# An audio tower on one core: centring as a matmul, experts two ahead, and a written order of all steps

## What is computed

```python
h = ln(patches @ W.T + b) * gamma + beta                 # 64 clips x 45 tokens x 64
h = h + attention(ln(h))                                 # 8 heads of 8, 4 kv heads, rotary, causal
h = h + sum_e cw[:, e] * (gelu(ln(h) @ W1[e] + b1[e]) @ W2[e] + b2[e])   # 8 experts, top 2 of a softmax gate
h = h + rwkv(ln(h))      # r, k, v, decay w, a, gate g from mixes with the token before; a state recurrence
                         # S = S*decay + (S @ -kk)(kk*a)^T + v k^T over 45 tokens; group norm; o*g @ W_o
h = h + ffn(ln(h))       # relu(x @ Wi.T + bi), two layers with a shared and a routed 128x128 matrix per clip
```

## Time and profile before

| | before |
|---|---|
| median of 3 runs (365.42 to 366.38) | 366.18 us |
| the profiled execution, its own time | 367.88 us |
| its span, first to last instruction | 365.1 us |
| PE matmul, busy | 316.4 us, 87% |
| DVE, busy | 214.6 us, 59% |
| ACT, busy | 192.1 us, 53% |
| POOL, busy | 138.8 us, 38% |
| mean granted TensorE clock | 0.949 |

### The profile page before, as it was taken

One profiled execution on the slowest core, in us unless ns is written; L12 is line 12 of the kernel. 1 busy time (PEld: TensorE's weight loads), 2 busy tenths in 40 slices (PEclk: granted clock), 3 DMA queues, 4 the chain that ended last, 5 costly groups with the idle time before them and its releaser, 6 DMA issues.

```text
span 365.1 us, 11788 instructions
## 1 busy us (share of the span) xinstructions
PE 316.4 (87%) x4888; PEld 221.0 (61%) x4888; DVE 214.6 (59%) x438; ACT 192.1 (53%) x378; POOL 138.8 (38%) x142
## 2 busy tenths in 40 slices
PE   4999899999998799999748895897787879969996
PEld 1446567766865544445324453897686869934784
DVE  4669987787556753332597389983566603285102
...
DMA packets 20556, 14.80 MB, mean 41 GB/s; under 512 B 2328, under 2 KB 19352, under 8 KB 20376
## 3 DMA queue, kind: packets, MB, share of 16 engines
...
...
HBM read 13.32 MB, written 0.74 MB: 38 GB/s over the span
## 4 chain that ended last, share of the span: by engine, by line
PE 62%; DVE 20%; ACT 9%; POOL 5%; issue 4%; DVEq 0%; POOLq 0%
PE PS L786 57%; PE PS L849 5%; DVE arena L591 2%; DVE arena L574 2%; POOL arena L342 2%; ACT arena L379 2%; ACT arena L376 2%; DVE arena L737 1%; POOL arena L338 1%; ACT arena L488 1%; DVE arena L731 1%; POOL arena L337 1%; DVE PS L523 1%; ACT arena L492 1%; ACT arena L371 1%
## 5 line engine op out<-in xcount | busy, mean ns | idle before, releaser
L786 PE MATMUL PS<-arena,K 128*128 128x360 f32 (+2 forms) x576 | 143.5, 503 | 21.3 <-DVE arena L591 6.7
L786 PE MATMUL PS<-arena 128*45 128x45 f32 (+5 forms) x3392 | 119.7, 223 | 18.1 <-issue 7.7
L786 PEld LDWEIGHTS PS<-arena,K 128*128 128x128 f32 (+2 forms) x576 | 74.8, 183 | 84.7 <-issue 22.8
L786 PEld LDWEIGHTS PS<-arena 128*45 128x45 f32 (+4 forms) x3392 | 102.4, 129 | 36.0 <-issue 13.4
L321 POOL TENSOR_TENSOR arena<-arena 128x360 f32<-128x360 f32 x32 | 29.4, 950 | 57.8 <-DVE arena L698 57.8
L698 DVE TENSOR_TENSOR arena<-PS,arena 128x360 f32<-128x360 f32 x32 | 16.9, 531 | 28.3 <-PE PS L786 26.7
L403 ACT COPY arena<-PS 128x360 f32<-128x360 f32 x32 | 14.8, 467 | 24.2 <-PE PS L849 24.2
L347 POOL TENSOR_TENSOR arena<-arena 128x360 f32<-128x360 f32 x4 | 4.4, 1111 | 56.3 <-DVE arena L582 56.3
L421 ACT ACTIVATE arena<-PS,K 128x720 f32<-128x720 f32 x32 | 24.9, 861 | 0.0
L310 POOL TENSOR_TENSOR arena<-arena,K 128x360 f32<-128x360 f32 x32 | 24.1, 789 | 0.0
L488 ACT ACTIVATE arena<-arena,K 128x360 f32<-128x360 f32 x8 | 4.3, 589 | 35.1 <-DVE arena L768 35.1
...
## 6 DMA issues: line engine op xcount, KB each, us to landing
WG<-wr SPq DMA_DIRECT2D x64, 64.0 KB, 1.9
arena<-wr SPq DMA_DIRECT2D x64, 64.0 KB, 1.8
...
```

The costliest lines, as they stand in the source:

```text
L786: return nc.tensor.matmul(o, l, r, start=start, stop=stop)
```

## The change

- A constant matrix `cent` (identity minus `mean`) is added to the first group of constants. `mean.k` multiplies by it, so that bank 0 holds the centred values; ACT squares from the bank, and the multiplication in `var.k` reads the bank. The DVE subtraction is gone.
- `hid.i` waits for `y_mul` of expert i-2 and for `cwb` of expert i-1; gelu alternates between slots 6, 7 and slots 17, 18 (`G_`). `y.i` waits for the gelu of expert i+1, and `cwT` for that of expert 1.
- `schedule()` is replaced by a written table of all 437 steps, the same ones, in which the chunks are at different steps at a time. A few waits that used the rank n of a step now name the chunk's step.

```diff
-    [("tokA", 64), ("tokB", 64), ("mean", 128), ("vecs", 36)],
+    [("tokA", 64), ("tokB", 64), ("mean", 128), ("cent", 128), ("vecs", 36)],
...
+G_ = (slot(6), slot(17))
...
+TABLE = """
+tok.0:01 mean.0:0 tok.0:2 mean.0:1 var.0:0 tok.0:3 mean.0:2 var.0:1 mean.0:3 var.0:2 mean.1:0 var.0:3 mean.1:1 var.1:0
+mean.1:2 var.1:1 mean.1:3 var.1:2 q.0:012 k.0:01 v.0:0 var.1:3 s.0:0 q.0:3 k.0:23 v.0:1 e.0:0 v.0:2 t.0:0 s.0:1 e.0:1
...
+mean.2:01 wo.0:3 var.2:0 mean.2:23 var.2:123 gate.0:0123 top2.0:0 hid.0:012 hid.1:0 hid.0:3 hid.1:123 cwT.0:012
...
+y.5:3 cb.6:3 y.6:12 hid.7:3 cb.7:12 y.7:1 mean.3:0 y.7:2 y.6:3 var.3:0 mean.3:1 cb.7:3 mixes.0:0 mean.3:2 var.3:1
+mixes.0:1 y.7:3 rk.0:0 var.3:2 vw.0:0 rk.0:1 mean.3:3 mixes.0:2 aw.0:0 var.3:3 rk.0:2 ab.0:0 vw.0:1 mixes.0:3 vw.0:2
+gh.0:0 aw.0:1 rk.0:3 aw.0:2 ab.0:1 gg.0:0 kk.0:0 gh.0:1 bon.0:0 vw.0:3 ab.0:2 kb.0:0 gg.0:1 aw.0:3 m.0:0 gh.0:2 kk.0:1
+m.1:0 bon.0:1 vt.0:0 gg.0:2 kb.0:1 ab.0:3 kk.0:2 lx.0:0 m.0:1 lt.0:0 gh.0:3 bon.0:2 lx.1:0 m.1:1 lt.1:0 gg.0:3 lx.2:0
+vt.0:1 kb.0:2 lt.2:0 lx.0:1 kk.0:3 m.0:2 lx.3:0 lt.0:1 bon.0:3 lt.3:0 m.1:2 lx.1:1 u.0:0 vt.0:2 kb.0:3 lt.1:1 y2.0:0
+lx.0:2 z.0:0 m.0:3 lx.2:1 w.0:0 m.1:3 lt.2:1 o.0:0 lx.3:1 vt.0:3 lt.0:2 lx.0:3 mean.4:0 lt.3:1 lt.0:3 lx.1:2 var.4:0
...
+u.0:2 lt.3:3 r.0:0 y2.0:2 u.0:3 o.0:1 y2.0:3 z.0:2 mean.4:1 z.0:3 w.0:23 var.4:1 o.0:23 mean.4:23 var.4:2 ro.0:1
+var.4:3 r.1:0 mean.5:1 ro.0:2 var.5:1 ro.0:3 mean.5:2 f.0:1 mean.5:3 var.5:2 r.0:1 f.0:2 var.5:3 fo.0:0 r.0:2 f.0:3
+r.1:1 r.0:3 r.1:23 fo.0:123
+"""
...
                 elif name == "mean":
-                    xc, sq = NORM_SLOTS[LNS[i]]
+                    sq = NORM_SLOTS[LNS[i]][1]
                     act.wait_ge(sem["ln_xc"], n)
-                    s.activation(a(c, sq), a(c, xc), ACT.Square).then_inc(sem["ln_sq"], 1)
+                    s.activation(a(c, sq), bank(c, 0), ACT.Square).then_inc(sem["ln_sq"], 1)
...
-                    dve.wait_ge(sem["ln_mean"], n)
-                    v.tensor_tensor(a(c, NORM_SLOTS[LNS[i]][0]), a(c, src), bank(c, 0),
-                                    ALU.subtract).then_inc(sem["ln_xc"], 1)
...
-                    v.tensor_tensor(a(c, dst), a(c, xc), a(c, sq), ALU.mult).then_inc(sem["ln_out"], 1)
+                    v.tensor_tensor(a(c, dst), bank(c, 0), a(c, sq), ALU.mult).then_inc(sem["ln_out"], 1)
...
-                    mm(bank(c, 0), k("mean"), a(c, src)).then_inc(sem["ln_mean"], 1)
+                    mm(bank(c, 0), k("cent"), a(c, src)).then_inc(sem["ln_xc"], 1)
...
-                    pe.wait_ge(sem["gelu"], COUNT["hid", 0, c])
+                    pe.wait_ge(sem["gelu"], COUNT["hid", 1, c])
...
+                    elif i == 1:
+                        pe.wait_ge(sem["gelu"], COUNT["hid", 0, c])
                     else:
-                        pe.wait_ge(sem["y_mul"], COUNT["y", i - 1, c])
-                        pe.wait_ge(sem["cwb"], COUNT["cb", i, c])
+                        pe.wait_ge(sem["y_mul"], COUNT["y", i - 2, c])
+                        pe.wait_ge(sem["cwb"], COUNT["cb", i - 1, c])
...
-                    pe.wait_ge(sem["gelu"], COUNT["hid", i, c])
...
+                    pe.wait_ge(sem["gelu"], COUNT["hid", min(i + 1, E - 1), c])
+                    if i == E - 1:
+                        pe.wait_ge(sem["y_mul"], COUNT["y", i - 1, c])
...
+    z["cent"] = np.eye(128) - z["mean"]
```

More of the change, by code:

```diff
@@ new lines @@
+pv.1:2 e.3:1 s.2:3 t.3:0 e.2:3 pv.2:1 s.4:0 t.2:2 t.3:1 pv.1:3 s.4:1 e.4:01 s.3:2 e.3:2 pv.2:2 t.2:3 s.3:3 pv.3:01
+t.3:2 e.3:3 pv.2:3 t.4:0 s.5:0 s.4:2 e.4:2 pv.3:2 e.5:0 t.4:1 s.5:1 t.3:3 s.4:3 t.4:2 e.4:3 pv.3:3 e.5:1 s.5:2 t.4:3
+s.5:3 e.5:2 pv.4:0 e.5:3 pv.4:12 t.5:0 pv.4:3 s.6:0 e.6:0 pv.5:0 t.5:1 s.6:1 t.5:23 e.6:1 s.6:2 t.6:0 pv.5:1 e.6:2
+pv.5:2 s.6:3 s.7:0 t.6:1 s.7:1 e.7:0 e.6:3 t.6:2 pv.5:3 e.7:1 s.7:2 e.7:2 pv.6:0 t.6:3 pv.6:1 s.7:3 pv.6:2 t.7:0 e.7:3
+pv.6:3 t.7:1 pv.7:0 t.7:2 pv.7:1 attT.0:0 pv.7:2 t.7:3 attT.0:1 pv.7:3 wo.0:0 attT.0:2 wo.0:1 attT.0:3 wo.0:2
@@ new lines @@
+mean.2:01 wo.0:3 var.2:0 mean.2:23 var.2:123 gate.0:0123 top2.0:0 hid.0:012 hid.1:0 hid.0:3 hid.1:123 cwT.0:012
+cw2.0:0 b2.0:0 cwT.0:3 cw2.0:12 b2.0:1 cb.0:0 b2.0:2 y.0:0 cb.0:1 cw2.0:3 b2.0:3 cb.0:2 cb.1:0 y.0:1 cb.1:1 y.0:2
+cb.1:2 hid.2:0 cb.0:3 hid.2:1 y.0:3 y.1:0 cb.1:3 cb.2:0 hid.2:2 y.1:1 cb.2:1 hid.2:3 hid.3:0 y.1:2 cb.2:2 hid.3:1
+y.1:3 hid.3:2 y.2:0 cb.3:0 cb.2:3 y.2:1 cb.3:1 hid.4:0 y.2:2 hid.4:1 hid.3:3 y.3:0 cb.3:2 cb.4:0 y.3:1 y.2:3 cb.4:1
+cb.3:3 hid.5:0 hid.4:2 hid.5:1 y.4:0 cb.5:0 hid.4:3 y.3:2 cb.4:2 y.4:1 hid.6:0 y.3:3 cb.4:3 hid.5:2 cb.5:1 y.5:0
@@ new lines @@
+hid.5:3 cb.6:0 y.4:2 cb.5:2 hid.6:1 y.4:3 cb.5:3 hid.6:2 hid.7:0 hid.6:3 y.5:12 cb.6:12 y.6:0 cb.7:0 hid.7:12 y.7:0
+y.5:3 cb.6:3 y.6:12 hid.7:3 cb.7:12 y.7:1 mean.3:0 y.7:2 y.6:3 var.3:0 mean.3:1 cb.7:3 mixes.0:0 mean.3:2 var.3:1
+mixes.0:1 y.7:3 rk.0:0 var.3:2 vw.0:0 rk.0:1 mean.3:3 mixes.0:2 aw.0:0 var.3:3 rk.0:2 ab.0:0 vw.0:1 mixes.0:3 vw.0:2
+gh.0:0 aw.0:1 rk.0:3 aw.0:2 ab.0:1 gg.0:0 kk.0:0 gh.0:1 bon.0:0 vw.0:3 ab.0:2 kb.0:0 gg.0:1 aw.0:3 m.0:0 gh.0:2 kk.0:1
+m.1:0 bon.0:1 vt.0:0 gg.0:2 kb.0:1 ab.0:3 kk.0:2 lx.0:0 m.0:1 lt.0:0 gh.0:3 bon.0:2 lx.1:0 m.1:1 lt.1:0 gg.0:3 lx.2:0
@@ new lines @@
+vt.0:1 kb.0:2 lt.2:0 lx.0:1 kk.0:3 m.0:2 lx.3:0 lt.0:1 bon.0:3 lt.3:0 m.1:2 lx.1:1 u.0:0 vt.0:2 kb.0:3 lt.1:1 y2.0:0
+lx.0:2 z.0:0 m.0:3 lx.2:1 w.0:0 m.1:3 lt.2:1 o.0:0 lx.3:1 vt.0:3 lt.0:2 lx.0:3 mean.4:0 lt.3:1 lt.0:3 lx.1:2 var.4:0
+u.0:1 lx.1:3 y2.0:1 lt.1:23 lx.2:2 ro.0:0 lt.2:2 mean.5:0 lx.2:3 lx.3:2 var.5:0 lt.2:3 z.0:1 f.0:0 lt.3:2 lx.3:3 w.0:1
+u.0:2 lt.3:3 r.0:0 y2.0:2 u.0:3 o.0:1 y2.0:3 z.0:2 mean.4:1 z.0:3 w.0:23 var.4:1 o.0:23 mean.4:23 var.4:2 ro.0:1
+var.4:3 r.1:0 mean.5:1 ro.0:2 var.5:1 ro.0:3 mean.5:2 f.0:1 mean.5:3 var.5:2 r.0:1 f.0:2 var.5:3 fo.0:0 r.0:2 f.0:3
@@ L86, in schedule @@
+r.1:1 r.0:3 r.1:23 fo.0:123
+"""
 def schedule():
     order = []
[L89 to L138, removed]
+    for entry in TABLE.split():
+        step, chunks = entry.split(":")
+        name, i = step.split(".")
+        order += [(name, int(i), int(c)) for c in chunks]
     return order
@@ L420, in _ @@
                     act.wait_ge(sem["hid_mm"], n)
-                    s.activation(halves(a(c, slot(6), 2 * W)), both(c), ACT.Gelu,
+                    s.activation(halves(a(c, G_[i % 2], 2 * W)), both(c), ACT.Gelu,
                                  bias=k("b1", i, i + 1)).then_inc(sem["gelu"], 1)
@@ L564, in _ @@
                 n = COUNT[name, i, c]
[L565 to L572 removed]
+                if name == "var":
+                    out_, sq = NORM_SLOTS[LNS[i]]
+                    dst = out_ if LNS[i] in ("lt", "gn") else N_
                     dve.wait_ge(sem["ln_rs"], n)
[L574 removed]
+                    v.tensor_tensor(a(c, dst), bank(c, 0), a(c, sq), ALU.mult).then_inc(sem["ln_out"], 1)
                     if LNS[i] == "lt":
@@ L896, in _ @@
                     if i == 0:
-                        pe.wait_ge(sem["cwT"], n)
+                        pe.wait_ge(sem["cwT"], c + 1)
                     else:
@@ L902, in _ @@
                     if i == 0:
-                        pe.wait_ge(sem["b2_add"], n)
-                    pe.wait_ge(sem["gelu"], COUNT["hid", i, c])
+                        pe.wait_ge(sem["b2_add"], c + 1)
+                    pe.wait_ge(sem["gelu"], COUNT["hid", min(i + 1, E - 1), c])
+                    if i == E - 1:
+                        pe.wait_ge(sem["y_mul"], COUNT["y", i - 1, c])
                     for j in range(2):
-                        last = mm(bank(c, 0, W, 0, 64 * j, 64 * j + 64), k("w2", i * D, i * D + D), a(c, slot(6 + j)))
+                        last = mm(bank(c, 0, W, 0, 64 * j, 64 * j + 64), k("w2", i * D, i * D + D),
+                                  a(c, G_[i % 2] + j * W))
                     last.then_inc(sem["y_mm"], 1)
@@ L975, in _ @@
                 elif name == "lt":
-                    pe.wait_ge(sem["x_ev"], n)
+                    pe.wait_ge(sem["x_ev"], COUNT["lx", i, c])
                     for p in range(PP):
```

7 lines of the change are left out of this document (4 added, 3 removed).

## The result

The changed kernel takes 339.75 us (median of 4 runs, 339.33 to 343.06) beside 366.28 us for the kernel before: ratio 0.929, with an interval from 0.9223 to 0.9357. The forecast was 339. The profiled execution took 339.59 us, its span 337.5, where the sum said 340.5 and 337.7.

What follows compares the result with a forecast made beforehand. PE, busy 316.4 of 365.1 us, was taken as the engine that matters, losing most in 175.5 to 253.3. Gains 2.3 + 1.5 + 0.5 + 4.2 + 14.3 + 4.6 = 27.4 us gave 339 against the median; range 322 to 356.

Steps and rivals of the forecast that it cites:

- Centring, "3 us in the lockstep order": Six layer norms: one DVE operation of 0.53 us off each chain, 3 us in lockstep, not added separately.
- Attention, 1.5: Attention, 24.4 to 98.0: PE idles 2.45 us, of which the new order gives back 1.5.
- rival E: Attention and experts: close dependent PE steps leave hand-overs uncovered, 52 use up the gain, 80 give 381 us; chance 0.06.
- Experts, 4.2: Experts two ahead: 2.6 us from hid.1 under top2, 1.6 us from seven rounds by 0.23.
- 175.5 to 317.3, 14.3: Recurrence layer: 62 + 3 + 62.5 = 127.5 us for 141.8, gain 14.3.
- 317.3 to 340.4, 4.6: Two norms, chunks 1 to 3 beside z, w, o and r.1:0: 4.6 of 8.1 us lost taken back.
- ACT, 60.8 us: First part of 175.5 to 317.3: ACT fullest with 50.55 us plus 10.3 of loads; with 1.2 filling, 62.
- A: The forecast itself: chunks apart, ACT filling the first half of the recurrence layer; 332 to 346 us, chance 0.52.
- B: 175.5 to 317.3: PE alone bounds, ACT and loads hide under chunk 0's matmuls; 327 us, chance 0.17.
- Rival C: Recurrence layer: each of 8 extra loads holds up the chunk PE waits for; 349 us, chance 0.20.
- POOL, 3 us for `add_shared`: Recurrence layer: four POOL instructions of 3.82 us hold DVE's products of kb, costing 3 us.
- Rival D: 175.5 to 317.3: in-order queues keep chunks together, that stretch stays, plus loads; 363 us, chance 0.05.

Runs made afterwards that it cites:

- the table early: Changed kernel with the written table's order only up to the end of the experts, lockstep order from norm 3 on: 362.42 us, ratio 0.988.
- the run on the lockstep order: Lockstep kernel with centring and two-ahead experts, but y, cb and hid of single chunks taking turns in the experts: 364.07 us, ratio 0.9954.
- putting the groups back: Changed kernel with its table rewritten from hid.0 to y.7, experts in groups of four chunks again: 336.6 us, ratio 0.9159.
- the lockstep with both edits: Kernel before plus the centring product and experts two ahead, lockstep order kept for all chunks: 358.07 us, ratio 0.9736.
- the table late: Changed kernel with lockstep order up to the end of the experts, the written table's order only from norm 3 on: 339.49 us, ratio 0.9237.
- Centring alone: Kernel before with only the centring product added, lockstep order and experts one ahead: 362.49 us, ratio 0.9857.
- two ahead alone: Kernel before with only the experts two ahead, subtraction in the norms and lockstep order kept: 361.26 us, ratio 0.9856.
- the other run: Changed kernel meant to lose eight table loads, but holding seven more, placed ahead of single activations: 349.35 us, ratio 0.9532.

## Why the prediction was right

The total is right within a microsecond; its terms are not all, and that their errors cancel so closely is luck.

- **Centring, "3 us in the lockstep order", inside the sums.** Right: 2.6. The square was overpriced: 464 ns, not 540, 1.8 us of ACT over 24.
- **0 to 24.4, 2.3.** Right: `q.0:0` starts at 22.0 on PE for 24.45, some 2.5. The 3.2 of the table of events is the DVE product, which stood further back in DVE's queue.
- **Attention, 1.5; 98.0 to 113.5, 0.5.** Failed. From the start of `q.0:0` on PE to `top2` it is 89.8 us for 89.05, so 0.8 lost for 2.0 forecast. By the rows of events attention alone would be 2.9 longer, but most of that is the `attT` that moved into it. PE's idle time there is 3.2 us for 3.3, with one wait of 1.2 us for DVE and one of 0.9 for ACT: the idle time that the order was to win is still there, in other places, and PE's busy time is 0.9 longer, some of it because the clock falls ahead of `top2` here. The uncovered hand-overs of rival E are there, then, but too few.
- **Experts, 4.2.** Right as a sum for the edit (4.1 in the lockstep order), wrong in the split: no round got shorter. Wrong for the change as a whole, because the step "the order costs the experts nothing" was never written down. The table gives the 4 us and more away again (5.3 with the table early), by alternating forms, as the run on the lockstep order shows; putting the groups back wins 3.7 of span.
- **175.5 to 317.3, 14.3, and 317.3 to 340.4, 4.6.** From the last `y_mul` to the last `fo` the kernel before takes 187.5 us, the lockstep with both edits 181.9, and with the table late 163.0: the order gives 18.9, and the forecast said 18.9 with the centring in it. Centring alone takes 2.8 off this part (184.7), two ahead alone 1.8 (185.7). Together 24.5 for 18.9 in the kernel with the table late: the sum was too low here by 5.6 us. In the changed kernel it must have been low by some 8, since the part up to the gate fell short by 2.6 and the experts by 5.4, if they cost there what they cost with the table early. The step that missed most of it is "I leave these", said of PE's gaps without a named cause in 253.3 to 317.3: they were 7.7 us before, and are 0.6 in the changed kernel and 0.2 with the table late.
- **ACT, 60.8 us, as the fullest engine of 62 us.** The failed term. In 173.9 to 216.0 ACT has 36.22 us of 42.1, hardly more than PE's 36.01 and DVE's 35.42. Taking 10.1 us off ACT gains 1.9, not the 4 and more of an engine that sets the pace. The truth lies between A and B: the extra loads slid under chunk 0's matmuls for four fifths. Rival C is refuted for these eight; the seven of the other run, at other places, did cost about their length.
- **POOL, 3 us for `add_shared`.** Not there: it held up no product. Moved to another place it costs 2.6, of the mechanism that was named.
- **The drain.** Refuted, as the forecast had it. The timeline of ACT:

```profile
200.84 1.28 ACT L339 ACT_TABLE_LOAD   x1
202.13 0.50 ACT L440 ACTIVATE arena<-arena 128x360 f32<-128x360 f32 x1
```

The load ends at 202.12, and the next activation starts at 202.13; all 13 loads are 16.7 us. "ScalarE: Activation LUTs" of the Trainium skill, section What ACT_TABLE_LOAD costs, has another 1.38 us for each; the trace disagrees.

- **The signs named.** No subtraction, 13 loads, a clock near 1 and no idle ACT behind a load: as said. PE busy "near 300": it is 315.2, because the order adds some 12 us of busy time to the 300 that the clock would have left, and the forecast had nothing for that. ACT fuller than PE up to the first `lt`: by 0.2 us only. And things that were to prove the forecast wrong did happen: a pair of `hid` and `y` takes 1.56 us for 1.30, so that an expert round is longer than before, and from `q.0:0` to the gate it is 0.8 us longer. The total held because the recurrence layer gave more.
- **Rival D** is out: the late half of the table alone is worth 18 us.

What stays open: why the late half of the table adds 6 us of busy time, and the clock's share of the 27.6, which has an upper estimate of 13 us and no experiment of its own.
